# Fusing the attention weights ahead of the second embedding, and a later split of the tokenizer's bias, in the first rounds of an audio tower kernel

## The reference

```python
# tokenizer
y = jnp.einsum('bpi,di->bpd', patches, W) + b
mu = jnp.mean(y, axis=-1, keepdims=True)
var = jnp.mean(jnp.square(y - mu), axis=-1, keepdims=True)
h = (y - mu) * jax.lax.rsqrt(var + EPS) * gamma + beta
# attention on layernorm(h)
q, k, v = x @ Wq.T + bq, x @ Wk.T + bk, x @ Wv.T + bv
out = softmax(q @ k.T / scale) @ v
# experts on layernorm(h + out): top two of six, three matmuls each, weighted sum, residual
```

## Time and profile before

| | |
|---|---|
| median of 3 runs | 1299.24 us (1298.17 to 1303.66) |
| profiled execution | 1298.97 us, span 1297.2 us |
| TensorE busy | 1222.9 us (94%) |
| VectorE busy | 1060.5 us (82%) |
| ScalarE busy | 843.3 us (65%) |
| GpSimd busy | 918.8 us (71%) |
| granted TensorE clock, mean | 0.984 |

### The profile page before, as it was taken

How to read it: one execution, slowest core, us unless ns; L and a number is a source line. 1 busy time by engine, 2 the same in 40 slices (tenths; PEclk the granted TensorE clock), 3 DMA queues, 4 the chain that set the end, 5 groups by cost and what they waited for, 6 DMA issues and landing times. The chain is left out here.

```text
span 1297.2 us, 28243 instructions
## 1 busy us (share of the span) xinstructions
PE 1222.9 (94%) x7888; PEld 1075.9 (83%) x7888; DVE 1060.5 (82%) x3593; ACT 843.3 (65%) x1838; POOL 918.8 (71%) x740
## 2 busy tenths in 40 slices
PE   4999999999999999999898999999999999999993
PEld 4888888888888888888677888888888888889883
DVE  5789999999999999998777778777777777878783
ACT  2677677667667757776655667676666666666662
POOL 2127777877777777787788777777676767767776
PEclk8899999999999999999999999999999999999997
DMA  4224555544444444554469989766696687687745
GB/s 133 83 85 126 146 144 150 138 116 115 120 118 115 126 112 109 156 167 123 118 182 203 255 188 234 134 114 127 112 236 108 125 193 154 108 185 164 128 55 60
DMA packets 137193, 180.45 MB, mean 139 GB/s; under 512 B 38345, under 2 KB 103501, under 8 KB 137037
## 3 DMA queue, kind: packets, MB, share of 16 engines
q0 software_dynamic: 75456, 69.19, 32.9%
q1 hardware_dynamic: 60316, 108.67, 27.5%
q10 hardware_dynamic: 1264, 0.79, 0.2%
HBM read 159.01 MB, written 101.49 MB: 201 GB/s over the span
## 5 line engine op out<-in xcount | busy, mean ns | idle before, releaser
L559 POOL DMA_INDIRECT out<-yo,tail x268 | 434.2, 1620 | 168.8 <-issue 138.1
L510 POOL DMA_INDIRECT expert_rows<-rec,row_i x256 | 354.7, 1386 | 72.6 <-issue 59.4
L979 ACT ACTIVATE h2v<-bank,small 128x512 f32<-128x512 f32 x134 | 92.3, 690 | 204.6 <-PE bank L777 203.3
L804 PE MATMUL bank<-w_sb,h_hi 128*128 128x256 f32 x1072 | 208.8, 288 | 4.1 <-issue 3.6
L777 PE MATMUL bank<-x_hi,w_sb 128*128 128x512 f32 x536 | 178.6, 395 | 5.7 <-DVE x_lo L1337 4.8
L777 PE MATMUL bank<-h_hi,w_sb 128*128 128x512 f32 x536 | 177.4, 392 | 1.4 <-issue 1.4
L804 PEld LDWEIGHTS bank<-w_sb,h_hi 128*128 128x128 f32 x1072 | 171.6, 191 | 4.9 <-issue 4.2
L804 PE MATMUL bank<-w_sb,h_lo 128*128 128x256 f32 x536 | 151.7, 283 | 0.0
L777 PEld LDWEIGHTS bank<-x_hi,w_sb 128*128 128x128 f32 x536 | 101.8, 190 | 27.5 <-issue 5.0
L777 PEld LDWEIGHTS bank<-h_hi,w_sb 128*128 128x128 f32 x536 | 101.0, 188 | 21.4 <-issue 1.7
L985 ACT ACTIVATE yo<-yo,gcol 128x256 f32<-128x256 f32 x268 | 113.9, 498 | 4.7 <-DVE yo L1368 4.7
(11 more groups left out here) (190 smaller groups left out, 3113.3 us busy)
## 6 DMA issues: line engine op xcount, KB each, us to landing
w_sb<-split_weights SPq DMA_DIRECT2D x189, 512.0 KB
xg<-expert_rows SPq DMA_DIRECT2D x67, 530.0 KB, 4.7
out<-h SPq DMA_DIRECT2D x32, 496.0 KB
split_weights<-half_w SPq DMA_DIRECT2D x36, 256.0 KB, 4.1
small<-in_esmall SPq DMA_DIRECT2D x67, 134.0 KB
x_in<-in_x SPq DMA_DIRECT2D x32, 250.0 KB, 10.7
expert_rows<-pad_rows SPq DMA_DIRECT2D x9, 530.0 KB, 9.1
raw_w<-in_eweights SPq DMA_DIRECT2D x36, 128.0 KB, 4.1
```

The source lines that it names most:

```text
L510: pool.indirect_dma_start(rows_dram, bass.IndirectOffsetOnAxis(ap=row_i[0:TOK, slot, j, k:k + 1], axis=0), rec[0:TOK, slot, j, :], None).t ...
L559: pool.indirect_dma_start(out, bass.IndirectOffsetOnAxis(ap=tail[:, t % TAILS, j, E8:].bitcast(I32), axis=0), yo[:, t % YO, j, :], None, c ...
L804: mm = pe.matmul(banks[6 + b][:, (j % 2) * D:(j % 2 + 1) * D], act[:, c, j * P:(j + 1) * P], w[:, 2, c, wh, :], start=(c == 0 and p == 0), ...
L979: act.activation(h2v[:, m, :], banks[bank + m][:], ACT.Relu, bias=small[:, t % SLOTS, DC + m:DC + m + 1]).then_inc(S["h2_v"], 1)
```

## The change

The function `fold` is cut in two on both engines, and the first part, `fold_weights`, is put earlier. On TensorE it stands in round 0 ahead of the embedding of group 1, and `fold_rest` behind it. On VectorE it stands in round 0 behind the statistics of group 0's `h`, followed by `nmr` of group 0 (now a function, `shifts`); `xT_lo`, `half_w` and group 1's statistics and `y` come behind it, then `fold_rest`. VectorE's wait for the constants ahead of the reciprocal goes; the one in round -1 stands ahead of it. In the later rounds `shifts` stays where `nmr` was.

At the start the wait for the tokenizer's weights no longer includes its bias: a semaphore of its own, `tok_bias_loaded`, is waited for by ScalarE behind group 0's `xT_hi`, and VectorE makes the low half of the bias behind `xT_lo`. TensorE starts the first embedding when the low half of the weights is there, and waits for the bias's low half before each bias product of that round.

The diff, with the semaphore's declaration and its count left out:

```diff
-                sp.dma_start(bias_raw["tok"][r:r + 1, :], tok_b).then_inc(S["tok_loaded"], 16)
+                sp.dma_start(bias_raw["tok"][r:r + 1, :], tok_b).then_inc(S["tok_bias_loaded"], 16)
...
-            def fold():
-
-                one = ones_r[:].bitcast(F32)
+            one = ones_r[:].bitcast(F32)
+
+            def fold_weights():
+
                 pe.wait_ge(S["const_loaded"], N_CONST)
...
                 mm.then_inc(S["fold_ps"], 1)
+
+            def fold_rest():
+
                 pe.wait_ge(S["fold_sb"], 9)
...
+                if it == 0:
+                    fold_weights()
                 if xa:
                     g, slot, rnd = xa
                     pe.wait_ge(S["xT_high"], g + 1)
                     pe.wait_ge(S["xT_low"], g + 1)
                     if it == -1:
-                        pe.wait_ge(S["proj_low"], 2)
+                        pe.wait_ge(S["proj_low"], 1)
...
+                            if it == -1:
+                                pe.wait_ge(S["proj_low"], 2)
                             mm = pe.matmul(into, ones_r[:, 0:TOK], bias_row["tok"][:], start=False, stop=True)
                         mm.then_inc(S["tok_ps"], 1)
                 if it == 0:
-                    fold()
+                    fold_rest()
...
-            act.wait_ge(S["tok_loaded"], N_TOK)
-            act.wait_ge(S["pool_const"], 2)
+            act.wait_ge(S["tok_loaded"], 16)
             high_halves("tok")
-            high_bias("tok")
...
                     act.activation(xT_hi[:], x_in[:, slot, :], ACT.Identity).then_inc(S["xT_high"], 1)
+                if it == -2:
+                    act.wait_ge(S["tok_bias_loaded"], N_TOK_BIAS)
+                    act.wait_ge(S["pool_const"], 2)
+                    high_bias("tok")
...
-            v.wait_ge(S["tok_loaded"], N_TOK)
-            v.wait_ge(S["pool_const"], 16)
+            v.wait_ge(S["tok_loaded"], 16)
             low_halves("tok", 1)
-            low_bias("tok", 3)
...
-            def fold():
+            def fold_weights():
 
                 s = S["fold_sb"]
+                v.reciprocal(invs_col[:], scale_col[:]).then_inc(S["invs"], 1)
                 v.wait_ge(S["fold_ps"], 1)
...
                                     invs_col[:, 0:1], ALU.add, ALU.mult).then_inc(s, 1)
+
+            def fold_rest():
+
                 v.wait_ge(S["fold_ps"], 2)
...
+                if it == 0:
+                    fold_weights()
+                    shifts(0)
...
+                if it == -2:
+                    low_bias("tok", 3)
+                    v.wait_ge(S["pool_const"], 16)
...
-                if x0:
-                    g, slot, rnd = x0
-                    v.wait_ge(S["rstd2"], g * 2 + 2)
-                    v.scalar_tensor_tensor(out=nmr[R, 0, :], in0=mv[R, 1, :, 0], scalar=-1.0, in1=rstd[R, 1, :],
-                                           op0=ALU.mult, op1=ALU.mult).then_inc(S["ln1"], 1)
+                if x0 and it > 0:
+                    shifts(x0[0])
...
                 if it == 0:
-                    v.wait_ge(S["const_loaded"], N_CONST)
-                    v.reciprocal(invs_col[:], scale_col[:]).then_inc(S["invs"], 1)
-                    fold()
+                    fold_rest()
                     low_halves("v", 4)
```

More of the change, by code:

```diff
@@ L204, in audio_tower @@
         S = {n: sem(n) for n in (
-            "tok_loaded", "const_loaded", "pool_const", "dve_const", "invs", "proj_high", "proj_low", "bias_zero",
+            "tok_loaded", "tok_bias_loaded", "const_loaded", "pool_const", "dve_const", "invs", "proj_high", "proj_low", "bias_zero",
             "w_high", "w_low", "dummy_cleared", "xT_high", "xT_low", "xn1T_low", "tok_ps", "ln1", "rstd1", "rstd2", "rstd3", "xn1_ready", "xn1T_ps", "xn1T_sb",
@@ L220, in audio_tower @@
         y_added = [sem(f"y_added{i}") for i in range(2)]
-        N_TOK = 16 * 3
+        N_TOK_BIAS = 16 * 2
         N_CONST = 16 * 13
@@ L1190, in step, with shifts @@
                     rows_low(1)
+            def shifts(g):
+                v.wait_ge(S["rstd2"], g * 2 + 2)
+                v.scalar_tensor_tensor(out=nmr[R, 0, :], in0=mv[R, 1, :, 0], scalar=-1.0, in1=rstd[R, 1, :],
+                                       op0=ALU.mult, op1=ALU.mult).then_inc(S["ln1"], 1)
             def choose_early(g, slot, rnd):
```

## The result

| | before | after |
|---|---|---|
| median of 12 runs each | 1299.2 us | 1289.22 us (1287.29 to 1291.99) |
| ratio | | 0.9928, 95% interval 0.9918 to 0.9938 |
| profiled execution, its span | 1298.97, 1297.2 us | 1288.87, 1287.1 us |
| first product with `q_proj`, the yardstick | 41.72 us | 33.35 us |

What follows compares the result with a forecast made beforehand. TensorE, busy 94% of the span, was taken as the bound. The terms moved the first `q_proj` product from 41.72 to 34.0, a gain of 7.7 us: 1298.97 - 7.7 = 1291.3, with 0.27 for the median 1291.5; range 1289.4 to 1296.4.

Steps and rivals of the forecast that it cites:

- (a): Start, bias split late: first embedding starts 1.1 us earlier, bounds 0.6 and 1.36.
- (b): First embedding's end: 0.9 us of the earlier start arrives there, depending on when the clock rises; bounds 0.3 and 1.36.
- (c): TensorE's weights' products run from 13.7 to 18.2 us, embedding 1 follows; VectorE's second statistics end at 21.7.
- (d): VectorE's gap of 2.39 us takes the fusing, 21.7 to 24.4; group 1's statistics start at 26.1, 0.6 us earlier.
- (e): TensorE's second fusing step runs from 24.4 to 28.5 us; embedding 2 starts at 28.8 instead of 36.69, when `y` is read.
- (f): Embedding 2, the third embedding, starts at half clock and takes 5.2 us, ending at 34.0; ends 3.3 and 6.2.
- (g): Next late before the query product: VectorE's low halves, ready at 32.5, 1.5 us ahead of TensorE's 34.0.
- B: Rival at the start: the clock holds through TensorE's holes, embedding 2 at full clock; gain 9.2 us, 1290.0; chance 0.14.
- A: Rival at the turn between the phases: one more half-clock stretch gives back 2.65 us, 1294.2; chance 0.25.
- D: Rival at the start: fusing at half clock, embedding 1 ends at 28.3; gain 1.9 us, 1297.3; chance 0.07.
- C: Rival in the steady rounds, slower: TensorE's 17.8 us wait for `rec` doubles, 10.1 us lost, 1309.3; chance 0.04.
- what I held against it: Objection to the skill's clock rule, at the start: two levels agree; that any unbroken run of matmuls counts as sustained does not.

Runs made afterwards that it cites:

- e2: The changed kernel with the bias put back to the start, so only the fusing is moved, on both engines; ratio to the kernel before 0.9917.
- The second pair: The kernel before and the changed kernel, each profiled once more without edits; ratios to the kernel before 1.0005 and 0.9927.
- e8: The changed kernel profiled once more, no edit; ratio to the kernel before 0.9927.
- e1: The kernel before with the late split of the bias alone, the fusing at its old place; ratio to the kernel before 0.9988.
- e9: The changed kernel with 24 extra matmuls in TensorE's last hole and the expert weights' chunks starting a round later; ratio to the kernel before 0.9917, median 1286.93 us.
- e5: The changed kernel with 24 extra matmuls of 256 columns filling TensorE's last hole; ratio to the kernel before 0.9926.
- e6: The changed kernel with 40 extra matmuls right ahead of the first product with `q_proj`, a pure delay; ratio to the kernel before 0.9969.
- e10: The same edit as e2 once more (changed kernel, bias back at the start); ratio to the kernel before 0.993.
- e3: The kernel before with the fusing moved on TensorE alone, VectorE in its old order, bias at the start; ratio to the kernel before 0.9965.

## Why the prediction was right

**The mechanism, and the place.** I forecast a gain of 7.7 us and 1291.5; measured are 9.4 by the ratio, which makes 1289.9 of 1299.24, and a median of 1289.2, which is 0.2 below the low end of my range. The direction and the mechanism held: a gain ahead of the yardstick stays. The attention products of groups 20, 28 and 29 in the kernel before show it (start, duration):

```profile
436.96 1.89 PE L722 MATMUL bank<-v_sb,pT 125*124 125x256 f32 x8
...
588.32 1.89 PE L722 MATMUL bank<-v_sb,pT 125*124 125x256 f32 x8
...
607.46 1.89 PE L722 MATMUL bank<-v_sb,pT 125*124 125x256 f32 x8
```

And in the changed kernel:

```profile
428.68 1.89 PE L730 MATMUL bank<-v_sb,pT 125*124 125x256 f32 x8
...
580.61 1.89 PE L730 MATMUL bank<-v_sb,pT 125*124 125x256 f32 x8
...
597.98 1.89 PE L730 MATMUL bank<-v_sb,pT 125*124 125x256 f32 x8
```

The lead is 8.37 us at the yardstick, 8.28 at group 20, 7.71 at group 28, and then 9.48 at group 29. That last step is no work of the change: between the two products lies the stretch at half clock of the kernel before, 600 to 603.4, which costs half its length, 1.7, and which the changed kernel didn't have in this execution. e2, which has one of its own (592.5 to 596), steps by nothing there: 7.95 and 7.92. At the end the spans are 10.1 apart. So of a gain near 10 some 8.4 is the mechanism, 0.7 more than I had, and the rest came behind the yardstick, for the most part where the clock happened to fall in one execution and not in the other. The second pair says the same: the mean gain at the yardstick is 8.9 us. Part of the distance between 7.7 and 9.4 is therefore an error of the sum, part is chance.

**(a) Bias.** 1.1 forecast, 1.28 found: `tok_proj` at 5.84, 0.27 behind the table load, so the weights' DMA landed nearer to the good end. In the mean of six profiles each the first matmul is at 8.19 with the late split and at 9.37 without, 1.2. The later work hid: no wait of TensorE stands at the first bias product.

**(b) The clock in the first embedding** was the widest term. S moved by 0.25 in the first profile, since the clock rose only at the embedding's end, by 1.07 in e8, by 1.37 in e1, by 0.19 in e9 and not at all in e5 (15.96 against 15.92). My bounds, 0.3 to 1.36, let the clock rise at 13 or earlier; in the first profile, e5 and e9 it rose at about 14, which I had no case for. The mean of six profiles each moved by 0.7, so the 0.9 was a little high, and the first profile was 0.65 short of it.

**(c), (d)** came as written: weights' products of 4.45 us from 14.11 to 18.56 with no wait for the constants, second embedding at full clock, reciprocal at 22.27 (21.7 said, later by what (b) fell short), group 1's statistics at 26.45 (26.1). Counted from S the statistics came 10.8 us later, where my sum has 11.1; this 0.3 came in all six profiles with both halves moved and the chunks in their place.

**(e)** Third embedding at 29.11 instead of 28.8. Of its two conditions `y` decides: the embedding starts 13.4 us behind S in six profiles, at either clock. Here TensorE was done with the transposes just then, so that no wait is shown. In e2, e6 and e10, with the clock up in the fusing's second step, it waits 0.70 to 1.00 us for `y`.

**(f) The third embedding** took 4.24 us in the first profile (29.11 to 33.35), not 5.2: the clock, at 0.50 up to 29 us, reads 0.75 on the mean of 29 to 33, so it came back some 2 us into the embedding, where it had needed 3.5 before. The same work took 4.78 in e8 and 5.36 in e6, up to its delay; with e2 and e10 the mean of five is 5.0. So the term was well sized, and the first profile was lucky in it. Within that profile the sum of the steps is 7.7 - 0.65 (S) + 0.3 (d) + 1.0 (f) = 8.35, and the yardstick says 8.37. For the changed kernel's three executions up to the yardstick (33.35, 33.06, and 33.77 in e6) the mean is 33.4, where I had 34.0.

The two rows of e8:

```profile
28.28 0.76 PE L573 MATMUL bank<-tok_proj,xT_hi 128*124 128x256 f32 x2
...
33.06 0.39 PE L573 MATMUL bank<-xn1T_hi,q_proj 128*128 128x496 f32 x1
```

And the start of the same embedding in e6:

```profile
28.41 0.76 PE L573 MATMUL bank<-tok_proj,xT_hi 128*124 128x256 f32 x2 [0.70 <-DVE y L1193]
```

**(g)** VectorE was ready at 32.7, 0.65 ahead of TensorE; I had 1.5. e5 shows it as what is late next.

**The rivals.** B (the clock holds, 1290.0) did not happen, though the measured time is nearer to its number than to mine: the clock fell in the hole of 2.8 us. Forced to hold in e5 it gave 0.5 to 1.6 us against the three executions above, where I had 1.5 (9.2 against 7.7). A (part given back at the turn) did not happen in this pair, whose changed profile has one stretch at half clock between 590 and 700 us (638 to 645) where the one of before has two. The place is able to give or take such a sum: measured against the first profile of before, the lead of e8 grows from 8.7 at group 20 to 13.6 at the last tile, that of e10 from 5.9 to 6.8, and that of e6 goes from 3.3 to 3.1. D fell: the clock was up at 13.98 and the second embedding quick. In e8 that embedding ran mostly at half clock (0.59 on the mean of 17 to 21 us), and still Q - S was only 0.5 longer than in the first profile, as VectorE's own queue covers it. C fell: TensorE's waits for `rec` from 34 to 640 us are 15.7 us in 67 and 2.6 in 15 more put down to no one, 18.3 in all against 17.8.

```profile
PE bank L673 <- ACT rec L883: 15.7, 67, 1.1
...
PE bank L673 <- issue: 2.6, 15, 0.2
```

**The rule of the Trainium skill** ("TensorE: Matmul & The Clock Gate", section "Part 1: The HAM clock gate"): its two levels are again the only ones that a stretch settles on. The second half of what I held against it is supported too: in the changed kernel TensorE is busy without a gap from 24.93, with products of one column and transposes, and the clock is at 0.50 from 25 to about 31.

**Open.** Why two profiles of the kernel before have the same half-clock stretch behind 600 us, and of the changed kernel neither has it, while e1, e2 and e10 have one between 592 and 602 and e3 to e6 and e9 have none, is not settled. The mean span - Q of before, 1254.8, is 1.9 above that of all the others, 1252.9, which spread by 5.0; whether an earlier start makes the turn shorter or two profiles of before are too few is not shown.

## What to carry to other kernels

Find the instant from which the bounding engine no longer waits, and count a change at the start by what it does to that instant alone. Where a chain crosses two in-order queues, move it in both: here each half alone brought the third embedding forward by 1.8 us, both together by 7.3. Put work into a gap that another engine's slowness makes, and behind it ask at once which queue is late next; it was 0.65 us away.

## What the hardware showed beyond that

The clock was the largest unknown of a change that never meant to touch it. From the first matmul to S, always the same 28 matmuls and what hangs on them, twelve profiles took 6.20 to 7.55 us; the third embedding, where the clock was not held, took 4.24 to 5.70. One profile of each kernel therefore says little about a term of half a microsecond. A hole of 2.8 us was enough for the clock to fall (0.86 on the mean of 22 to 25 us, 0.50 behind), though TensorE had been busy for 14 us before it; 24 matmuls of 256 columns without use in that hole kept it at 1.00 through the light products behind. In e8 it fell with hardly a hole at all: TensorE was busy from 8.05 on, the weights' products, 16 of their 28 matmuls of one column, ran from 12.71 to 17.24, and behind a hole of 0.31 us the second embedding found the clock at 0.50 from 18 us on.
